# Making each head's softmax shift on GpSimd instead of VectorE, and turning and dividing its sums two units later

## The chip, the cores and the metric

One core of one Trainium2 chip. The metric is the device time of one launch in microseconds (us), the median of several runs. The profile is one execution of the program, taken by the hardware profiler. Engines: PE is TensorE (PEld its weight loads), DVE is VectorE, ACT is ScalarE, POOL is GpSimd, SP is SyncE, which issues DMAs here.

## The reference

A graph attention layer with a residual and a layer norm, then three relational graph convolutions with a residual and a layer norm, over 1250 nodes of 768 features and 40000 edges. The change lies in the attention alone:

```python
hh = h.reshape(n, 12, 64)
ft = jnp.einsum('nhd,ed->nhe', hh, W_fc)
a1 = jnp.einsum('nhd,hd->nh', ft, attn_l)
a2 = jnp.einsum('nhd,hd->nh', ft, attn_r)
e = jax.nn.leaky_relu(a1[src] + a2[dst], negative_slope=0.2)
m = jax.ops.segment_max(e, dst, num_segments=n)
ee = jnp.exp(e - m[dst])
denom = jax.ops.segment_sum(ee, dst, num_segments=n)
alpha = ee / denom[dst]
agg = jax.ops.segment_sum(alpha[:, :, None] * ft[src], dst, num_segments=n)
res = jnp.einsum('nhd,ed->nhe', hh, W_res)
return jax.nn.relu((res + agg).reshape(n, 12 * 64))
```

The maximum m only shifts the exponent: the kernel must take it from each node's incoming edges, and a node without edges must come out finite.

## The kernel before

A first stage counts the edges between each pair of nodes into dense matrices and projects the nodes; the last stage does the three convolutions as dense products. Neither is touched. Between them stands `attention`, which treats the graph as a dense matrix: for each of 12 heads (H) and each of 10 tiles (NT) of 125 source nodes (T) there is one **unit** u = head x 10 + tile, a matrix of 125 source nodes by 1250 destination nodes. The five engines run their own programs, written out by hand, and meet at semaphores. For unit u, in the order in which its data pass:

- `lift` (ACT, L644): y = relu(0.8 (a2 + a1)), 125x1250, into one of YS = 5 buffers. ACT lifts unit u + 4 behind the exponent of unit u, and waits until the pw of the buffer's last user is done.
- `bend` (POOL, L620), "the addition": y = y + lowb, where lowb is the shift of the head, spread over 125 partitions.
- `exponent` (ACT, L650): y = exp(y + a1_low).
- `weights` (DVE, L727), "pw": pw = min(y, 1) x edge counts, into one of 3 buffers.
- `gather` (PE, L791): six matmuls add x (64 features and a one) times pw into head_sums.

Once a head: `keep_sums` (ACT, L655) copies the sums out of PSUM behind exponent 1 of the next head, `turn_sums` (PE, L802) multiplies them by the projection, `divide` (DVE, L732 to L737) divides by the sum of weights into `share`, and `add` (POOL, L627), "the addition of a head", adds share to the result, behind the bend of unit 7.

The shift. `spread` (PE, L772) spreads a1 of a head over PSUM. `best` (DVE, L699), "the lookup", finds for one tile of destination nodes the largest a1 among their sources, one column of `tops` each; ten lookups give a head's maxima. DVE does the lookup of unit u + 20 beside the pw of unit u, two heads ahead; at tile 9 it stands before the pw, so that the lookups of tiles 8 and 9 follow each other. `lows` (DVE, L705 to L715) makes from the ten columns the shift 0.2 a2 - leaky(top + a2), with nodes without edges set to zero by a comparison with -GONE: four operations on 125x10 numbers, each behind a wait on the one before. `turn_low` (PE, L780) turns the 125x10 columns, `keep_low` (DVE, L721), "the row copy", copies them to SBUF, and SP writes them to memory and spreads them into `lowb` (L567, L571), two buffers. The order by hand puts lows(h + 2) behind the pw of tile 9 of head h, turn_low(h + 1) in front of the gather of tile 0, keep_low(h + 1) behind the pw of tile 0, turn_sums(h - 1) behind the gather of tile 0, divide(h - 1) behind the lookup of tile 3. Before unit 0, DVE does lows(0) behind ten lookups and lows(1) behind ten more; POOL waits only for the spread shift of head 0.

The tiles are named in the profile: y, pw, tops, bias_steps (the steps of the shift), low_cols (the shift), low_rows (turned), low_spread (lowb), head_sums, head_out, share, res. Buffer numbers are left out there (a2_col is a_col).

## Time and profile before

| | us |
|---|---|
| median of 3 runs (lowest, highest) | 2604.76 (2603.11, 2607.9) |
| the profiled execution's own time | 2603.86 |
| its span, first to last instruction | 2602.1 |
| PE busy | 2227.9 |
| DVE busy | 1376.9 |
| ACT busy | 785.4 |
| POOL busy | 540.9 |

The span is what the rows of the profile are placed in, from 0 us. A row of the timeline gives start and duration, engine, line and operation, output and inputs, and in brackets the idle time of the engine before it with the instruction that ended it. An engine that has taken up an instruction and waits for something inside the chip, not for a semaphore, counts as busy. Mean granted clock of PE over the span is 0.937 of full.

### The profile page before, as it was taken

The page shows a single profiled execution, that of the slowest core. Times are in us where ns is not written, and L with a number is a line of the kernel's source. Part 1 is how long each engine was busy: PE and PEld are TensorE (multiplying, and loading weights), DVE is VectorE, ACT ScalarE, POOL GpSimd, SP SyncE. Part 2 cuts the span into 40 slices and gives each one's busy share as a digit, 9 for nine tenths or more (in the row PEclk, how much of TensorE's full clock was granted, in tenths as well). Part 3 has the DMA queues.
Part 4 walks back from the last instruction along what each step waited for, and adds up shares of the span by engine and source line. Part 5 has one row for each costly group of instructions (what it writes and reads, how often), then busy time and mean ns, then how long its engine had stood idle before and what let it go on. Part 6 is the DMA issues. An engine that isn't in the chain of part 4 may idle for free.

```text
span 2602.1 us, 29664 instructions
## 1 busy us (share of the span) xinstructions
PE 2227.9 (86%) x10953; PEld 1849.4 (71%) x10954; DVE 1376.9 (53%) x1942; ACT 785.4 (30%) x1040; POOL 540.9 (21%) x224
## 2 busy tenths in 40 slices
PE   3997743777777745999999999999999989999997
PEld 1555531232323315999999989999999989999997
DVE  7886637999999956223333234232232242334335
ACT  0132222666666633112122133121121231212212
POOL 0000003989899930000000000000000000000000
PEclk9998875979889877999999999999999999999999
DMA  0133332211111043232343332333332342344332
GB/s 17 50 85 89 88 88 64 96 34 39 38 36 45 14 111 112 75 110 85 106 121 87 113 102 67 98 111 98 90 109 90 106 118 89 104 119 124 104 106 77
DMA packets 139392, 222.22 MB, mean 85 GB/s; under 512 B 86848, under 2 KB 87086, under 8 KB 139269
## 3 DMA queue, kind: packets, MB, share of 16 engines
q1 hardware_dynamic: 99935, 154.48, 20.9%
q0 software_dynamic: 39344, 66.16, 9.0%
q8 instruction: 80, 1.31, 0.2%
q14 instruction: 33, 0.27, 0.0%
HBM read 189.76 MB, written 30.56 MB: 85 GB/s over the span
## 4 chain that ended last, share of the span: by engine, by line
PE 55%; DMA 4%; DVE 2%; ACT 2%; issue 0%; SPq 0%; ACTq 0%; DVEq 0%
PE banks L1036 28%; PE banks L1008 26%; DMA w_raw<-in_L_gnn_w_root_dram 3%; DVE w_lo L1277 1%; ACT w_hi L1156 1%; DMA s_x<-x_tiles 1%; PE banks L1071 0%; DMA emb_raw<-in_L_gnn_w_rel_dram 0%; PE banks L1045 0%; PE banks L1058 0%; PE banks L1089 0%; DVE h_lo L1308 0%; DVE tail_stats L1327 0%; ACT accT L1184 0%; DVE back L1325 0%
## 5 line engine op out<-in xcount | busy, mean ns | idle before, releaser
L1008 PE MATMUL banks<-ct_in,h_hi 125*128 125x416 f32 (+1 forms) x1710 | 604.3, 353 | 0.6 <-ACT accT L1141 0.6
L1008 PE MATMUL banks<-ct_in,h_lo 125*128 125x416 f32 (+1 forms) x1710 | 603.1, 353 | 0.0
L1036 PE MATMUL banks<-g_hi,w_hi 128*128 128x416 f32 (+1 forms) x1440 | 515.9, 358 | 24.2 <-DVE g_lo L1299 24.2
L1036 PE MATMUL banks<-g_hi,w_lo 128*128 128x416 f32 (+1 forms) x1440 | 512.6, 356 | 0.0
L1036 PE MATMUL banks<-g_lo,w_hi 128*128 128x416 f32 (+1 forms) x1440 | 511.4, 355 | 0.0
L1277 DVE TENSOR_TENSOR w_lo<-w_raw,w_hi 128x768 fp32r<-128x768 f32 (+1 forms) x228 | 227.9, 1000 | 469.8 <-ACT w_hi L1156 469.8
L620 POOL TENSOR_TENSOR y<-y,low_spread 125x1250 f32<-125x1250 f32 x120 | 426.1, 3582 | 69.8 <-ACT y L644 38.0
L791 PE MATMUL head_sums<-pw,x 125*65 125x512 f32 x720 | 316.1, 587 | 101.9 <-DVE pw L727 100.7
L1156 ACT CAST w_hi<-w_raw 128x768 fp32r<-128x768 f32 (+1 forms) x228 | 197.9, 869 | 452.4 <-PE banks L1036 355.5
L1008 PEld LDWEIGHTS banks<-ct_in,h_lo 125*128 125x128 f32 x1710 | 323.7, 189 | 4.2
L1008 PEld LDWEIGHTS banks<-ct_in,h_hi 125*128 125x128 f32 x1710 | 322.4, 189 | 4.1 <-ACT accT L1141 0.8
L791 PEld LDWEIGHTS head_sums<-pw,x 125*65 125x65 f32 x720 | 102.2, 153 | 305.8 <-issue 170.7
L1287 DVE TENSOR_TENSOR gs<-banks,inv 128x416 f32<-128x416 f32 (+3 forms) x180 | 106.6, 592 | 392.4 <-PE banks L1008 392.3
L1172 ACT CAST g_hi<-gs 128x416 fp32r<-128x416 f32 (+3 forms) x180 | 97.5, 542 | 701.4 <-DVE gs L1287 701.4
L976 POOL DMA_DIRECT2D inv<-s_inv x27 | 15.4, 572 | 1386.6 <-DVE gs L1287 1372.9
L1036 PEld LDWEIGHTS banks<-g_hi,w_hi 128*128 128x128 f32 x1440 | 275.4, 191 | 33.2 <-DVE w_lo L1277 22.7
L727 DVE SCALAR_TENSOR_TENSOR pw<-y,csum 125x1250 f32<-125x1250 f32 x120 | 283.2, 2369 | 3.9 <-PE head_sums L791 2.8
L1036 PEld LDWEIGHTS banks<-g_lo,w_hi 128*128 128x128 f32 x1440 | 274.1, 190 | 4.7
L1036 PEld LDWEIGHTS banks<-g_hi,w_lo 128*128 128x128 f32 x1440 | 274.2, 190 | 3.3
L292 DVE TENSOR_SCALAR oh_key<-iota_key,edge_cols,minus_window 125x750 bf16<-125x750 uint16 x516 | 211.3, 474 | 80.4 <-PE win L417 55.3
L644 ACT ACTIVATE y<-a_spread,a_high 125x1250 f32<-125x1250 f32 x120 | 160.2, 1338 | 193.7 <-DVE pw L727 158.4
L417 PE MATMUL win<-oh_key,oh_rem 125*128 125x375 bf16 x1032 | 200.7, 340 | 11.1 <-issue 8.2
(175 smaller groups left out, 1592.9 us busy)
## 6 DMA issues: line engine op xcount, KB each, us to landing
w_raw<-in_L_gnn_w_rel_dram SPq DMA_DIRECT2D x117, 384.0 KB, 3.2
ct_in<-s_ct POOLq DMA_DIRECT2D x18, 2031.2 KB, 27.9
w_raw<-in_L_gnn_w_rel_dram SPq DMA_DIRECT2D x54, 448.0 KB, 4.2
ct_in<-s_ct POOLq DMA_DIRECT2D x9, 2041.0 KB, 28.9
s_ct<-ct_stage SPq DMA_DIRECT2D x30, 610.4 KB
w_raw<-in_L_gnn_w_root_dram SPq DMA_DIRECT2D x39, 384.0 KB, 3.3
w_raw<-in_L_gnn_w_root_dram SPq DMA_DIRECT2D x18, 448.0 KB, 5.8
a_spread<-s_a SPq DMA_DIRECT2D x12, 610.4 KB
```

The source lines that it names most:

```text
L292: nc.vector.tensor_scalar(oh_key[:, p, b], iota_key[:].rearrange("e s r d -> e (s r d)"), edge[:, 1, bass.ds(c, 1)], minus_w[:, bass.ds(w, ...
L417: ins = nc.tensor.matmul(win[:, p, m, 0:BANK * KEY], oh_rem[:, bass.ds(q, 1), :, b].rearrange("e q s -> e (q s)"), oh_key[:, p, b, m * BAN ...
L620: nc.gpsimd.tensor_tensor(y[:, u % YS], y[:, u % YS], lowb[:, h % 2], ALU.add).then_inc(bent, 1)
L644: nc.scalar.activation(y[:, u % YS], a2b[:, h % 2], ACT.Relu, scale=1.0 - SLOPE, bias=a1_high[:, s, h:h + 1]).then_inc(risen, 1)
L727: nc.vector.scalar_tensor_tensor(out=pw[:, u % 3], in0=y[:, u % YS], scalar=1.0, in1=csum[:, u % NT], op0=ALU.min, op1=ALU.mult).then_inc( ...
L791: ins = nc.tensor.matmul(po[:, o:o + w], x[:, s, h], pw[:, u % 3, o:o + w], start=s == 0, stop=s == NT - 1)
L1008: ins = nc.tensor.matmul(pb[0:rows, PA, 0:s.w], a, b, start=j == 0, stop=j == len(pairs) - 1)
L1036: ins = nc.tensor.matmul(pb[:, m, 0:s.w], a, b, start=s.first and j == 0, stop=s.last and j == len(parts) - 1)
L1156: nc.scalar.copy(w_hi[:, s.wi % WS, 0:s.mt * 128], w_raw[:, s.wi % 2, 0:s.mt * 128]).then_inc(w_hi_done, 1)
L1172: nc.scalar.copy(g_hi[0:rows, s.gi % 2, 0:s.w], gs[0:rows, 0:s.w]).then_inc(g_hi_done, 1)
L1277: nc.vector.tensor_tensor(w_lo[at], w_raw[:, s.wi % 2, 0:s.mt * 128], f32(w_hi[at]), ALU.subtract).then_inc(w_lo_done, 1)
L1287: nc.vector.tensor_tensor(gs[0:rows, 0:s.w], pb[0:rows, PA, 0:s.w], inv[0:rows, s.slab % 2, 0:s.w], ALU.mult).then_inc(gs_done, 1)
```

## The change

The shift is made by POOL. `lows` moves into POOL's program and is written there in operations on two tensors, or on one with constants: eight operations on 125x10 numbers in place of four, six steps buffers in place of three. The wait for the maxima stands in front of them. lows(0) and lows(1) stand before POOL's first bend; lows(h + 1) stands in front of the bend of tile 2 of head h, for h from 1 to 10. On PE, turn_low(h + 1) now stands behind the gather of tile 1, and turn_sums(h - 1) behind that of tile 2. On DVE, keep_low(h + 1) stands behind the pw of tile 2, and divide(h - 1) behind the lookup of tile 5. POOL's addition of a head stays behind bend 7.

```diff
--- before.py
+++ after.py
@@ -513,7 +513,7 @@
         wfc = sb("wfc", [HD, HD], F32)
         wfcT = sb("wfcT", [HD + 1, HD + 1], F32)
         tops = sb("tops", [T, NU], F32)
-        steps = sb("bias_steps", [T, 3, NT], F32)
+        steps = sb("bias_steps", [T, 6, NT], F32)
         low = sb("low_cols", [T, 2, NT], F32)
         row = sb("low_rows", [NT, T], F32)
         den = sb("den", [T, 2, NT // 2], F32)
@@ -626,8 +626,31 @@
                 at = res[:, :, h * HD:(h + 1) * HD]
                 nc.gpsimd.tensor_tensor(at, share[:].rearrange("p m t f -> p (m t) f"), at, ALU.add).then_inc(res_added, 1)
 
+            def lows(h):
+                a2, at, n = a2_col[:, :, h], [steps[:, j] for j in range(6)], h * 7
+                pool.wait_ge(maxed, (h + 1) * NT)
+                pool.wait_ge(low_ready, h)
+                nc.gpsimd.tensor_tensor(at[0], tops[:, h * NT:(h + 1) * NT], a2, ALU.add).then_inc(bias_step, 1)
+                nc.gpsimd.tensor_scalar(at[5], a2, SLOPE, None, ALU.mult).then_inc(bias_step, 1)
+                pool.wait_ge(bias_step, n + 1)
+                nc.gpsimd.tensor_scalar(at[1], at[0], 0.0, 1.0 - SLOPE, ALU.max, ALU.mult).then_inc(bias_step, 1)
+                nc.gpsimd.tensor_scalar(at[2], at[0], SLOPE, None, ALU.mult).then_inc(bias_step, 1)
+                pool.wait_ge(bias_step, n + 4)
+                nc.gpsimd.tensor_tensor(at[3], at[1], at[2], ALU.add).then_inc(bias_step, 1)
+                nc.gpsimd.tensor_scalar(at[4], at[0], -GONE, None, ALU.is_gt).then_inc(bias_step, 1)
+                pool.wait_ge(bias_step, n + 6)
+                nc.gpsimd.tensor_tensor(at[3], at[3], at[4], ALU.mult).then_inc(bias_step, 1)
+                pool.wait_ge(bias_step, n + 7)
+                if h >= 2:
+                    pool.wait_ge(low_turned, h - 1)
+                nc.gpsimd.tensor_tensor(low[:, h % 2], at[5], at[3], ALU.subtract).then_inc(low_ready, 1)
+
+            lows(0)
+            lows(1)
             for u in range(NU):
                 h, s = divmod(u, NT)
+                if s == 2 and 1 <= h and h + 1 < H:
+                    lows(h + 1)
                 bend(u)
                 if s == 7 and h:
                     add(h - 1)
@@ -699,22 +722,6 @@
                 nc.vector.tensor_tensor_reduce(junk[:, u % 2], a1[:, 0:N], nbr[:, t], 1.0, -NOEDGE / 10,
                                                ALU.subtract, ALU.max, tops[:, u:u + 1]).then_inc(maxed, 1)
 
-            def lows(h):
-                a2, at = a2_col[:, :, h], [steps[:, n] for n in range(3)]
-                dve.wait_ge(maxed, (h + 1) * NT)
-                nc.vector.tensor_tensor(at[0], tops[:, h * NT:(h + 1) * NT], a2, ALU.add).then_inc(bias_step, 1)
-                dve.wait_ge(bias_step, h * 3 + 1)
-                nc.vector.scalar_tensor_tensor(out=at[1], in0=at[0], scalar=SLOPE, in1=at[0],
-                                               op0=ALU.mult, op1=ALU.max).then_inc(bias_step, 1)
-                dve.wait_ge(bias_step, h * 3 + 2)
-                nc.vector.scalar_tensor_tensor(out=at[2], in0=at[1], scalar=-GONE, in1=at[1],
-                                               op0=ALU.is_gt, op1=ALU.mult).then_inc(bias_step, 1)
-                dve.wait_ge(bias_step, h * 3 + 3)
-                if h >= 2:
-                    dve.wait_ge(low_turned, h - 1)
-                nc.vector.scalar_tensor_tensor(out=low[:, h % 2], in0=a2, scalar=SLOPE, in1=at[2],
-                                               op0=ALU.mult, op1=ALU.subtract).then_inc(low_ready, 1)
-
             def keep_low(h):
                 dve.wait_ge(low_turned, h + 1)
                 dve.wait_ge(low_out, 16 * h)
@@ -739,28 +746,24 @@
 
             for t in range(NT):
                 best(t)
-            lows(0)
             best(NT)
             best(NT + 1)
             keep_low(0)
             node_tables()
             for t in range(2, NT):
                 best(NT + t)
-            lows(1)
             for u in range(NU):
                 h, s = divmod(u, NT)
                 more = h + 2 < H
                 if s == NT - 1 and more:
                     best(u + 2 * NT)
                 weights(u)
-                if s == 0 and h + 1 < H:
+                if s == 2 and h + 1 < H:
                     keep_low(h + 1)
                 if s < NT - 1 and more:
                     best(u + 2 * NT)
-                if s == 3 and h:
+                if s == 5 and h:
                     divide(h - 1)
-                if s == NT - 1 and more:
-                    lows(h + 2)
             divide(H - 1)
 
         @block.tensor
@@ -814,12 +817,12 @@
             spread(2)
             for u in range(NU):
                 h, s = divmod(u, NT)
-                if s == 0 and h + 1 < H:
-                    turn_low(h + 1)
                 if s == NT - 1 and h + 3 < H:
                     spread(h + 3)
                 gather(u)
-                if s == 0 and h:
+                if s == 1 and h + 1 < H:
+                    turn_low(h + 1)
+                if s == 2 and h:
                     turn_sums(h - 1)
             turn_sums(H - 1)
```

DVE at a boundary of heads: the pw of tile 9 (the second L699 in front of it is its lookup), then the next head. Before:

```order
L699 ISA junk,tops<-a_spread,nbr 125x1250 [waits maxed,a1_set]
L699 ISA tops 125x1
L727 SCALAR_TENSOR_TENSOR pw<-y,csum 125x1250 [waits summed_e,raised]
L705 TENSOR_TENSOR bias_steps<-tops,a_col 125x10 [waits maxed]
L707 SCALAR_TENSOR_TENSOR bias_steps<-bias_steps 125x10 [waits bias_step]
L710 SCALAR_TENSOR_TENSOR bias_steps<-bias_steps 125x10 [waits bias_step]
L715 SCALAR_TENSOR_TENSOR low_cols<-a_col,bias_steps 125x10 [waits low_turned,bias_step]
L727 SCALAR_TENSOR_TENSOR pw<-y,csum 125x1250 [waits summed_e,raised]
L721 COPY low_rows<-head_out 10x125 [waits low_out,low_turned]
L699 ISA junk,tops<-a_spread,nbr 125x1250 [waits maxed,a1_set]
L699 ISA tops 125x1
L727 SCALAR_TENSOR_TENSOR pw<-y,csum 125x1250 [waits summed_e,raised]
```

and with the change (pw is L734, the lookup L722, the row copy L728):

```order
L722 ISA junk,tops<-a_spread,nbr 125x1250 [waits maxed,a1_set]
L722 ISA tops 125x1
L734 SCALAR_TENSOR_TENSOR pw<-y,csum 125x1250 [waits summed_e,raised] x2
L722 ISA junk,tops<-a_spread,nbr 125x1250 [waits maxed,a1_set]
L722 ISA tops 125x1
L734 SCALAR_TENSOR_TENSOR pw<-y,csum 125x1250 [waits summed_e,raised]
L722 ISA junk,tops<-a_spread,nbr 125x1250 [waits maxed,a1_set]
L722 ISA tops 125x1
L734 SCALAR_TENSOR_TENSOR pw<-y,csum 125x1250 [waits summed_e,raised]
L728 COPY low_rows<-head_out 10x125 [waits low_out,low_turned]
L722 ISA junk,tops<-a_spread,nbr 125x1250 [waits maxed,a1_set]
```

The four operations between the two pw are gone, so these follow each other, and the row copy stands two pw further on.

POOL in heads 1 and 2, before (L620 is the bend, L627 the addition of a head; head 2 begins where low_in0 is waited for):

```order
L620 TENSOR_TENSOR y<-y,low_spread 125x1250 [waits low_in1,risen]
L620 TENSOR_TENSOR y<-y,low_spread 125x1250 [waits risen] x7
L627 TENSOR_TENSOR res<-share,res 125x10x64 [waits res_in,shared]
L620 TENSOR_TENSOR y<-y,low_spread 125x1250 [waits risen] x2
L620 TENSOR_TENSOR y<-y,low_spread 125x1250 [waits low_in0,risen]
L620 TENSOR_TENSOR y<-y,low_spread 125x1250 [waits risen] x7
```

and with the change, from the first bend of head 1:

```order
L620 TENSOR_TENSOR y<-y,low_spread 125x1250 [waits low_in1,risen]
L620 TENSOR_TENSOR y<-y,low_spread 125x1250 [waits risen]
L633 TENSOR_TENSOR bias_steps<-tops,a_col 125x10 [waits low_ready,maxed]
L634 TENSOR_SCALAR bias_steps<-a_col 125x10
L636 TENSOR_SCALAR bias_steps<-bias_steps 125x10 [waits bias_step]
L637 TENSOR_SCALAR bias_steps<-bias_steps 125x10
L639 TENSOR_TENSOR bias_steps<-bias_steps 125x10 [waits bias_step]
L640 TENSOR_SCALAR bias_steps<-bias_steps 125x10
L642 TENSOR_TENSOR bias_steps<-bias_steps 125x10 [waits bias_step]
L646 TENSOR_TENSOR low_cols<-bias_steps 125x10 [waits low_turned,bias_step]
L620 TENSOR_TENSOR y<-y,low_spread 125x1250 [waits risen] x6
L627 TENSOR_TENSOR res<-share,res 125x10x64 [waits res_in,shared]
```

Eight operations stand between the second and the third bend of the head, all others where they were.

PE at a boundary of heads, before: the gather of tile 9, the turned shift, the gather of tile 0, the turned sums:

```order
L791 MATMUL head_sums<-pw,x 65x512 [waits weighed]
L791 MATMUL head_sums<-pw,x 65x512
L791 MATMUL head_sums<-pw,x 65x226
L780 MATMUL head_out<-ident,low_cols 10x125 [waits shared,low_kept,low_ready]
L791 MATMUL head_sums<-pw,x 65x512 [waits o_kept,x_in1,weighed]
L791 MATMUL head_sums<-pw,x 65x512
L791 MATMUL head_sums<-pw,x 65x226
L802 MATMUL head_out<-wfcT,oT 125x65 [waits shared,low_kept,o_kept]
L802 MATMUL head_out<-wfcT,oT 125x65 x9
```

and with the change (the gather is L794, the turned shift L783, the turned sums L805), from the gather of tile 0:

```order
L794 MATMUL head_sums<-pw,x 65x512 [waits o_kept,x_in1,weighed]
L794 MATMUL head_sums<-pw,x 65x512
L794 MATMUL head_sums<-pw,x 65x226
L794 MATMUL head_sums<-pw,x 65x512 [waits weighed]
L794 MATMUL head_sums<-pw,x 65x512
L794 MATMUL head_sums<-pw,x 65x226
L783 MATMUL head_out<-ident,low_cols 10x125 [waits shared,low_kept,low_ready]
L794 MATMUL head_sums<-pw,x 65x512 [waits weighed]
L794 MATMUL head_sums<-pw,x 65x512
L794 MATMUL head_sums<-pw,x 65x226
L805 MATMUL head_out<-wfcT,oT 125x65 [waits shared,low_kept,o_kept]
L805 MATMUL head_out<-wfcT,oT 125x65 x9
```

The turned shift stands behind the gather of tile 1 and the turned sums behind that of tile 2.

## Rows read from the trace of the kernel before

**Rows 1.** The page: busy tenths in 40 slices of 65 us, DVE and POOL.
```profile
DVE  7886637999999956223333234232232242334335
...
POOL 0000003989899930000000000000000000000000
```

**Rows 2.** Busy time in a stretch: PE, PEld, DVE, ACT, POOL; clock, DMA, GB/s.
```profile
554.00:596.00 42.00, 35.55 (x88) 14.90 (x89) 41.83 (x39) 27.23 (x22) 38.36 (x12) 0.76 0.13 38
```

**Rows 3.** Timeline, DVE and POOL: start us, us, engine, line, operation, shapes.
```profile
620.99 2.27 DVE L727 SCALAR_TENSOR_TENSOR pw<-y,csum 125x1250 f32<-125x1250 f32 x1
623.18 1.45 DVE L699 CUSTOM_DVE_ANT_0 junk<-a_spread,nbr 125x1250 bf16<-125x1250 f32 x1
...
625.00 0.82 DVE L737 TENSOR_TENSOR share<-head_out,rden 125x640 f32<-125x640 f32 x1
...
647.51 2.81 DVE L705 TENSOR_TENSOR bias_steps<-tops,a_col 125x10 f32<-125x10 f32 x1
650.36 2.31 DVE L707 SCALAR_TENSOR_TENSOR bias_steps<-bias_steps 125x10 f32<-125x10 f32 x1
...
653.00 1.46 DVE L727 SCALAR_TENSOR_TENSOR pw<-y,csum 125x1250 f32<-125x1250 f32 x1
...
655.90 3.75 POOL L620 TENSOR_TENSOR y<-y,low_spread 125x1250 f32<-125x1250 f32 x1 [3.26 <-ACT y L644]
```

**Rows 4.** Timeline, POOL, additions of heads 4 and 5.
```profile
632.26 7.63 POOL L620 TENSOR_TENSOR y<-y,low_spread 125x1250 f32<-125x1250 f32 x2
...
639.85 12.80 POOL L620 TENSOR_TENSOR y<-y,low_spread 125x1250 f32<-125x1250 f32 x4
```

**Rows 5.** Timeline, DVE, the divisions of heads 10 and 11 and the end.
```profile
873.60 0.82 DVE L737 TENSOR_TENSOR share<-head_out,rden 125x640 f32<-125x640 f32 x1
...
913.09 0.82 DVE L737 TENSOR_TENSOR share<-head_out,rden 125x640 f32<-125x640 f32 x1
913.83 15.53 DVE L727 SCALAR_TENSOR_TENSOR pw<-y,csum 125x1250 f32<-125x1250 f32 x6
```

**Rows 6.** The row copy by source, 520 to 870 us: ns, first and last start.
```profile
L721 DVE COPY low_rows<-head_out x9: 270/270/271, 528.9 to 864.0; 10x125 f32<-10x125 f32 x9
```

**Rows 7.** Timeline, POOL: small operations, and an addition without pw.
```profile
5.64 0.12 POOL L198 MEMSET noedge_bias<- 125x1 f32 x1
5.68 0.22 POOL L199 MEMSET zero_a<- 125x128 bf16 x1
...
397.44 0.15 POOL L606 MEMSET emb_cols<- 128x67 f32 x1
397.65 1.13 POOL L608 MEMSET hot_rows<- 3x1250 f32 x1
...
433.86 2.40 POOL L620 TENSOR_TENSOR y<-y,low_spread 125x1250 f32<-125x1250 f32 x1
```

**Rows 8.** The head addition by source: ns min/median/max, first and last start.
```profile
L627 POOL TENSOR_TENSOR res<-share,res x12: 1531/2698/2768, 500.1 to 938.3; 125x640 f32<-125x640 f32 x12
```

**Rows 9.** Timeline, DVE and POOL, the start of head 0.
```profile
439.69 0.07 DVE L699 DVE_READ_ACCUMULATOR2_ANT tops<- 125x1 f32 x1
...
431.08 13.09 POOL L620 TENSOR_TENSOR y<-y,low_spread 125x1250 f32<-125x1250 f32 x5 [31.71 <-DMA low_spread<-s_low]
```

**Rows 10.** Timeline, DVE and POOL, head 0 to head 1.
```profile
482.69 1.45 DVE L727 SCALAR_TENSOR_TENSOR pw<-y,csum 125x1250 f32<-125x1250 f32 x1
486.81 0.28 DVE L721 COPY low_rows<-head_out 10x125 f32<-10x125 f32 x1 [2.66 <-PE head_out L780]
...
483.53 2.88 POOL L620 TENSOR_TENSOR y<-y,low_spread 125x1250 f32<-125x1250 f32 x1 [2.77 <-ACT y L644]
```

**Rows 11.** Timeline, PE: gathers of a unit, and the last ones.
```profile
637.69 2.31 PE L791 MATMUL head_sums<-pw,x 125*65 125x512 f32 x6 [1.70 <-DVE pw L727]
...
857.27 4.43 PE L791 MATMUL head_sums<-pw,x 125*65 125x512 f32 x6 [4.04 <-DVE pw L727]
...
926.67 6.51 PE L791 MATMUL head_sums<-pw,x 125*65 125x512 f32 x18 [1.26 <-DVE pw L727]
```

## The prediction

> **What bounds the kernel now.** The page comes first. In its 40 slices POOL is at 8 or 9 tenths in seven in a row, and DVE is at 9 there too [rows 1]: the attention stage, some 397 to 940 us, the only place the diff touches. Outside it nothing changes, so the sum is about this stage alone. There a stretch of 42 us, about a head, shows DVE busy for 41.83 and POOL for 38.36 us, PE for 35.55 and ACT for 27.23 [rows 2]. Two engines that are full side by side ask for the timeline. In it one weights operation (pw, L727) takes 1.46 us when POOL stands still and 2.27 us while POOL adds; the lookup for the maxima (L699) takes 1.45 us beside an addition [rows 3]. An addition of POOL (L620) takes 7.63 / 2 = 3.8 us where each meets a pw, and 12.80 / 4 = 3.2 us where only half of them do [rows 4]. So pw and the addition take turns at something they share, and nothing else does. I call it the port. The next look is the period: from 632.26 to 639.85 POOL starts two additions [rows 4], so a unit (one addition, one pw) costs 3.80 us of port. From the addition's end to pw's it is 1.3 us, which leaves 2.5 for POOL. That is the bound: not an engine but the turn-taking.
>
> How much of a head is port? In heads 10 and 11 there are neither lookups nor a new shift between the two divisions, and they are 913.09 - 873.60 = 39.49 us apart [rows 5]: ten units, and 1.49 for the addition of a head (L627, 1.4 us of port) and its hand-over. In the full heads the row copy L721 comes 9 times between 528.9 and 864.0 [rows 6]: 41.89 us a head. So 2.40 us a head are lost to the port. The boundary shows where: the first two shift operations stand in DVE for 2.81 and 2.31 us, waiting for a turn that they need for a moment, while POOL does two additions; then the y ring is empty, POOL waits 3.26 us for ACT's lift, which waits for pw [rows 3], and the port lies free for all of it but the 1.45 us of pw (L727 at 653.00), some 1.8 us, and for 0.35 us before that pw.
>
> **The change, part by part.** (1) Four DVE operations a head go (L705 to L715). They stand for 5.49 us in DVE (647.51 to 653.00) [rows 3], though only 2.15 us of that is port left idle later; the rest were turns in which POOL worked. Worth up to 2.40 us in each of the heads, all that is above 39.49.
>
> (2) Eight POOL operations a head come, of 125x10, each pair behind a wait on POOL's own result. Their port turns are short, but they run one behind another and the additions queue behind them. In that time DVE can use the port only if a pw is ready. Two are (the last of a head and the first of the next stand together in DVE's order now), and POOL waits for them, which is useful work. What is left, s, is port time lost. The trace has no such operation. From below: a memset and the next, which waits for it, start 0.21 us apart (L606, L608); without a wait they start 0.04 us apart (L198, L199) [rows 7]. Half of the eight wait. Four of each kind make 1.0 us; with only a memset's own 0.12 to 0.15 us for a waiting one it is 0.7. From above: the line through L627 alone (640 elements, 1.53 us [rows 8]) and the addition alone (1250, 2.40 us [rows 7]) leaves 0.62 us for an operation with no elements; eight make 5 us. With an addition of 2.88 us, one that starts after an idle [rows 10], it leaves 0.11 us, 0.9 us for eight. 
>
> (3) One more term comes with it: the addition behind the small ones starts after an idle (2.88, not 2.5 us [rows 10]): 0.35 us. A head then costs 39.49 + 1.3 + 0.35 = 41.14 us, 0.75 less than before.
>
> (4) The lead. POOL runs up to four additions ahead of DVE. Before, head 0 began its additions at 431.08, while DVE was still at the lookups of head 1; five were done at 444.17, just as the first pw became ready [rows 9]. Now the shift of head 1 stands in front of the first addition and needs the last of those lookups, which ends at 439.76 [rows 9]. POOL starts its additions at 439.76 + 1.3 = 441.1, has two done at 446.3, the first pw ends at 447.7, the ninth 8 x 3.80 later at 478.1. Two lookups in a row let POOL add twice (483.1), then come the pw of unit 9 (484.4), one small operation and that of head 1, unit 0: 486.0. Before, it ended at 482.69 + 1.45 = 484.14 [rows 10], and POOL was at its fifth addition of head 1 by then (the one at 483.53 that waits for the lift), three further on. Ten heads of 41.14 give 897.4 for the first pw of head 11. From there eight units and one more pw (31.8) and 1.5 for the addition of a head: 930.7. Before, the last pw ended at 929.36 [rows 5]. PE finished its backlog 3.8 us later (933.18) [rows 11]; now the last three pw come less bunched, 0.6 us back. The sum is **+0.7 us**: the gain of ten heads pays for the lead that is given up. Both ends are absolute times, so nothing is counted twice.
>
> (5) turn_low stands behind the gather of unit 1 now, keep_low behind the pw of unit 2. At 2.4 GHz a gather takes 2.31 us in a unit of 3.80 [rows 11], so unit 1's is over 1.5 us before pw 2 ends: free. At 1.2 GHz (the granted clock averages 0.76 of full in the stretch [rows 2]) a gather takes 4.43 us [rows 11] and DVE could wait some 2 us at keep_low, as it did once before, 2.66 us at 486.81 [rows 10]. I take nothing: the pause of 4.04 us in front of the last gather of a head, behind which the slow gather stands [rows 11], gets shorter.
>
> (6) turn_sums and divide go two units back, three units apart as before; POOL's head addition, still behind bend 7, now needs a division that comes after pw 5. While POOL is one addition ahead, bend 7 runs (2.2 to 2.7 us) beside lookup 5 and the division (2.57 us from pw's end to share's, 623.26 to 625.83 [rows 3]): no wait, as before. I take nothing, since the small operations of (2) bring the lead down to one in each head.
> (7) Loads, steps and semaphores: three more rows of 10 numbers in bias_steps; SP's order is unchanged, and from the row copy at unit 2 to the first use of the shift there are eight units less POOL's lead, over 20 us.
>
> The profiled execution took 2603.9 us around its span of 2602.1 and lies 0.9 us under the median of 2604.8. With +0.7 and a little for (5), I predict **2606 us**. About 0.2%, 5.2 us, is what a measurement of this kernel can tell from no change. The sum moves by 11 us for 1 us of s: it is slower than that from s = 1.7, faster below s = 0.75.
>
> **The rivals.** *Slower, POOL waits for the division.* If POOL comes to bend 7 two additions ahead, it has nothing to do until DVE is through lookup 5 and the division; the port is free for 2.57 us. For it: two lookups in a row at each boundary do give POOL a second addition, and the division was two units earlier before. Against: the eight operations take about one turn away again. It decides if POOL's lead at bend 7 is two or more. Price 2.6 us in ten heads: 2632 us. Chance 0.12.
> *Slower, the small operations are dear.* At 0.4 us each, between the two lines of (2), s = 3.2 and the time 2627 us. For it: the 1.53 us of L627 for half the elements of a 2.40 us addition [rows 7, 8]. Chance 0.13; the part of my own forecast with s just over 1.7 adds 0.02.
> *Faster, they hide or cost next to nothing.* If most of the eight slip through while pw 9 and pw 0 hold the port, s falls to 0.3 and the time to 2595 us. Against: L627 takes 1.53 us alone and 2.70 us in the median, so POOL operations that read do wait [rows 8]. Chance 0.08. Or they are cheap: if a waiting one takes no more than such a memset, s is the 0.7 us of (2) and the time 2599 us. For it: the 0.04 us between memsets [rows 7]; against: the 0.21 us with a wait. Chance 0.07.
> The section of the Trainium skill named in (2) leads to this last case.
> The change does what it says: the order shows the operations moved, so that is no rival of its own.
>
> **How the numbers follow.** Forecast 0.58 (within 5.2 us), faster 0.08 + 0.07 = 0.15, slower 0.12 + 0.13 + 0.02 = 0.27. The range leaves out the waiting division and the upper half of the dear operations at one end and half of the fast cases at the other: 2597 (s near 0.5) to 2619 (s near 2.4).
>
> **What would show it.** Right: the shift's operations on POOL in about 1.3 us plus waits of 1.4 us for pw; no 3.26 us idle of POOL at the boundary; L721 about 41.1 us apart; first addition at 441; DVE no longer at 41.8 of 42 but idle for short pieces, waiting for y; the last pw near 931. Wrong: an idle of 2 us and more in front of L627, waiting for share, a start-to-start time of the small operations far from 0.16 us, DVE waiting at the row copy for PE, or a lead that is won back.

## The result, and the profile after the change

| | before | after |
|---|---|---|
| time, median (us) | 2606.22 (2603.11 to 2607.90) | 2628.16 (2625.96 to 2631.24) |
| ratio after / before | | 1.0086 (95%: 1.0069 to 1.0104) |
| profiled execution: own time / span | 2603.9 / 2602.1 | 2627.3 / 2625.5 |
| first pw of head 0, of head 1, of head 11 ends | 445.97, 484.14, 901.55 | 447.77, 486.33, 915.11 |
| last pw ends | 929.36 | 948.06 |
| last addition of a head ends | 939.79 | 959.28 |

The kernel became 22 us slower. The forecast was 2606 with a range up to 2619: a miss, and not a close one. Of all the launches behind the numbers below, one of e1_add_late took 9581.64 us where its others took 2607.5 to 2611.5 us; it is left out of the interval, and why it was slow is not known. Here and below, "a head" is the time from the end of the pw of tile 0 to the end of the next one, read from the timelines. The busy tenths of the page after the change are the first place where it shows, beside [rows 1].

```profile
DVE  7886637988888846323233334232232342334335
...
POOL 0000003999999950000000000000000000000000
```

DVE has come down from 9 to 8 tenths in the attention stage and POOL has gone up to 9 in each slice: the work has moved as the diff says. Two stretches, a short head and a long one, say so in us. The columns are those of [rows 2].

```profile
554.00:596.00 42.00, 31.08 (x91) 11.93 (x89) 37.20 (x35) 27.45 (x21) 41.28 (x21) 0.92 0.14 40
596.00:640.00 44.00, 32.78 (x87) 12.41 (x86) 38.08 (x35) 26.64 (x21) 39.71 (x20) 0.84 0.11 34
```

POOL is now the engine with no room in the first (41.28 of 42), and has lost 4.3 us of 44 in the second. The row copy (by source; it answers to [rows 6]) gives the mean, and the head addition by source (it answers to [rows 8]) says what POOL lost:

```profile
L728 DVE COPY low_rows<-head_out x8: 270/270/277, 537.2 to 841.2; 10x125 f32<-10x125 f32 x8
```

```profile
L627 POOL TENSOR_TENSOR res<-share,res x12: 1530/2696/2775, 509.5 to 957.7; 125x640 f32<-125x640 f32 x12
its engine sat idle before it (us, times) until:
  DVE share L744: 33.1, 8
```

(841.2 - 537.2) / 7 = 43.43 us a head between these two copies, where 41.14 was forecast. POOL stands 33.1 us in front of the head addition, waiting for the division. The timelines break that up: five times 3.96 us, in heads 4, 5, 7, 8 and 9; twice 0.39 us, in heads 1 and 3; and the rest in front of the last one, where nothing queues behind. The ten heads from head 1 on last

41.30, 41.82, 41.30, **44.66, 43.79**, 41.83, **43.80, 44.66, 43.80**, 41.82 us.

So there are two kinds. The five short ones have a mean of 41.61, the five long ones (exactly those with the wait of 3.96 us) of 44.14. That is 2.53 us more, five times, 12.7 us. The small operations themselves are the other surprise. They stand in POOL's timeline at the start of head 0, where nothing disturbs them, with the addition behind them:

```profile
439.24 0.21 POOL L633 TENSOR_TENSOR bias_steps<-tops,a_col 125x10 f32<-125x10 f32 x1 [23.24 <-DVE tops L722]
439.42 0.26 POOL L634 TENSOR_SCALAR bias_steps<-a_col 125x10 f32<-125x10 f32 x1
439.64 0.28 POOL L636 TENSOR_SCALAR bias_steps<-bias_steps 125x10 f32<-125x10 f32 x1
...
440.21 0.20 POOL L639 TENSOR_TENSOR bias_steps<-bias_steps 125x10 f32<-125x10 f32 x1
...
441.11 0.21 POOL L646 TENSOR_TENSOR low_cols<-bias_steps 125x10 f32<-125x10 f32 x1
441.28 9.19 POOL L620 TENSOR_TENSOR y<-y,low_spread 125x1250 f32<-125x1250 f32 x3
```

The eight take s = 441.28 - 439.24 = 2.04 us, 0.26 us each, not the 1.3 us of term (2).

**How a long head comes about.** The timeline of head 4, whose boundary is at 602 to 616 us, PE first, then ACT, DVE and POOL:

```profile
603.05 4.43 PE L794 MATMUL head_sums<-pw,x 125*65 125x512 f32 x6 [4.04 <-DVE pw L734]
607.41 4.53 PE L775 MATMUL a_spread<-a_rows,ident 12*125 12x512 f32 x6
611.87 4.32 PE L794 MATMUL head_sums<-pw,x 125*65 125x512 f32 x6
...
616.23 1.20 ACT L678 COPY oT<-head_sums 65x1250 f32<-65x1250 f32 x1 [4.26 <-PE head_sums L794]
...
600.73 2.27 DVE L734 SCALAR_TENSOR_TENSOR pw<-y,csum 125x1250 f32<-125x1250 f32 x1 [2.71 <-ACT y L673]
...
611.98 1.46 DVE L722 CUSTOM_DVE_ANT_0 junk<-a_spread,nbr 125x1250 bf16<-125x1250 f32 x1 [1.22 <-PE a_spread L775]
...
619.92 3.08 DVE L734 SCALAR_TENSOR_TENSOR pw<-y,csum 125x1250 f32<-125x1250 f32 x1 [1.93 <-ACT y L673]
...
636.36 0.82 DVE L744 TENSOR_TENSOR share<-head_out,rden 125x640 f32<-125x640 f32 x1
637.10 1.45 DVE L734 SCALAR_TENSOR_TENSOR pw<-y,csum 125x1250 f32<-125x1250 f32 x1
...
612.48 20.82 POOL L620 TENSOR_TENSOR y<-y,low_spread 125x1250 f32<-125x1250 f32 x6
637.26 2.69 POOL L627 TENSOR_TENSOR res<-share,res 125x640 f32<-125x640 f32 x1 [3.96 <-DVE share L744]
```

Read it as a chain. (a) In front of the pw of tile 8 DVE waits 2.71 us for ACT's exponent: bend 8 stands behind the addition of a head, and DVE is through the units before it sooner than POOL. (b) So PE has nothing to gather for 4.04 us, in front of gather 8. From head 2 on this pause stands at every boundary, 4.04 to 4.05 us. The kernel before has no pause of that length in front of gather 8: with POOL four additions ahead, PE's pauses there were 1.3 to 1.7 us, those at the spread and at gather 9 0.4 and 1.2 us, and 4.04 us in front of gather 9 at one boundary alone, that of head 10, where no spread is left to be made [rows 11]. (c) From 602 on the granted clock is at half speed: gather 8, the spread for the lookups of a later head and gather 9 take 4.43, 4.53 and 4.32 us, and the three end 13.1 us after the pause (616.19), where DVE and ACT need them. (d) DVE's lookup waits 1.22 us for the spread; ACT's copy of the sums waits 4.26 us for gather 9, and the exponent of tile 2 stands behind that copy. (Before, that copy was done early: in heads 2 to 10 it started 2.3 to 3.5 us before the pw of tile 0 ended.) (e) The pw of tile 2 starts 9.16 us after that of tile 0 ended (610.76). (f) POOL goes on meanwhile, is done with bend 7 at 633.30, two additions ahead, and stands until the division, which now comes behind the pw of tile 5, has ended. From 634.61 to 637.10 nobody uses the port: 2.49 us, the length of the excess.

The short head before it, same views, 41.3 us earlier, has the same pause and another clock:

```profile
561.75 3.78 PE L794 MATMUL head_sums<-pw,x 125*65 125x512 f32 x6 [4.05 <-DVE pw L734]
565.47 2.36 PE L775 MATMUL a_spread<-a_rows,ident 12*125 12x512 f32 x6
568.13 4.01 PE L794 MATMUL head_sums<-pw,x 125*65 125x512 f32 x6 [0.30 <-DVE pw L734]
...
572.17 1.20 ACT L678 COPY oT<-head_sums 65x1250 f32<-65x1250 f32 x1 [1.50 <-PE head_sums L794]
...
576.08 2.72 DVE L734 SCALAR_TENSOR_TENSOR pw<-y,csum 125x1250 f32<-125x1250 f32 x1 [2.45 <-ACT y L673]
...
592.61 2.70 POOL L627 TENSOR_TENSOR res<-share,res 125x640 f32<-125x640 f32 x1 [0.39 <-DVE share L744]
```

Busy time of the two boundaries, with the columns of [rows 2]:

```profile
560.00:574.00 14.00, 10.56 (x20) 3.51 (x21) 13.63 (x12) 8.59 (x8) 13.67 (x12) 0.76 0.00 0
602.00:616.00 14.00, 12.95 (x18) 4.26 (x18) 12.78 (x10) 6.28 (x5) 13.67 (x12) 0.51 0.00 0
```

In the short one the clock came back for the spread (2.36 us), fell again for gather 9, and is 0.76 over the boundary, against 0.51, which is 1.2 GHz, all through the long one. ACT's copy starts 2.71 us after the pw of tile 0 ended (569.46), not 5.47 us, the pw of tile 2 starts 6.62 us after it, and POOL, whose bend 7 ends at the same distance in both (22.8 and 22.5 us), stands 0.39 us. Each of the five long heads follows a boundary with one piece of 13.7 us at the low level; each short one follows pieces of 3.4 or 6.8 us.

### The profile page after: what moved, and what is told of

Its sections match the earlier page's. It is cut to its first block, busy times and chain, and to the rows that moved or that the text cites. A ratio compares the mean times of both kernels' runs of the same rounds, so it can differ in the third digit from the quotient of the medians.

```text
span 2625.5 us, 29724 instructions
## 1 busy us (share of the span) xinstructions
PE 2230.7 (85%) x10953; PEld 1845.1 (70%) x10954; DVE 1331.2 (51%) x1894; ACT 788.0 (30%) x1040; POOL 570.2 (22%) x320
## 4 chain that ended last, share of the span: by engine, by line
PE 55%; DMA 4%; DVE 2%; ACT 1%; issue 0%; SPq 0%; ACTq 0%; DVEq 0%
PE banks L1039 28%; PE banks L1011 25%; DMA w_raw<-in_L_gnn_w_root_dram 3%; DVE w_lo L1280 1%; ACT w_hi L1159 1%; DMA s_x<-x_tiles 1%; PE banks L1074 0%; DMA emb_raw<-in_L_gnn_w_rel_dram 0%; PE banks L1048 0%; PE banks L1061 0%; PE banks L1092 0%; DVE h_lo L1311 0%; DVE tail_stats L1330 0%; ACT accT L1187 0%; DVE back L1328 0%
## 5 line engine op out<-in xcount | busy, mean ns | idle before, releaser
L1039 PE MATMUL banks<-g_hi,w_hi 128*128 128x416 f32 (+1 forms) x1440 | 516.8, 359 | 22.5 <-DVE g_lo L1302 22.5
L794 PE MATMUL head_sums<-pw,x 125*65 125x512 f32 x720 | 316.9, 585 | 137.8 <-DVE pw L734 122.1
L620 POOL TENSOR_TENSOR y<-y,low_spread 125x1250 f32<-125x1250 f32 x120 | 404.0, 3401 | 0.0
L794 PEld LDWEIGHTS head_sums<-pw,x 125*65 125x65 f32 x720 | 100.7, 153 | 348.5 <-issue 184.4
L734 DVE SCALAR_TENSOR_TENSOR pw<-y,csum 125x1250 f32<-125x1250 f32 x120 | 289.7, 2421 | 64.6 <-ACT y L673 63.6
L673 ACT ACTIVATE y<-y,a_low 125x1250 f32<-125x1250 f32 x120 | 159.8, 1331 | 137.7 <-POOL y L620 137.6
```

Source lines behind the costliest of these rows:

```text
L620: nc.gpsimd.tensor_tensor(y[:, u % YS], y[:, u % YS], lowb[:, h % 2], ALU.add).then_inc(bent, 1)
L673: nc.scalar.activation(y[:, u % YS], y[:, u % YS], ACT.Exp, bias=a1_low[:, s, h:h + 1]).then_inc(raised, 1)
L734: nc.vector.scalar_tensor_tensor(out=pw[:, u % 3], in0=y[:, u % YS], scalar=1.0, in1=csum[:, u % NT], op0=ALU.min, op1=ALU.mult).then_inc( ...
L794: ins = nc.tensor.matmul(po[:, o:o + w], x[:, s, h], pw[:, u % 3, o:o + w], start=s == 0, stop=s == NT - 1)
L1039: ins = nc.tensor.matmul(pb[:, m, 0:s.w], a, b, start=s.first and j == 0, stop=s.last and j == len(parts) - 1)
```

## The experiments

"After" is the changed kernel. Medians stand beside those of the kernel before on the same chip. Where the text compares two medians of different chips, the difference is good to some 2 us: counted from each chip's own kernel before, e1 is 17.5 us under after, not 19.3, e2 12.1, e5 4.6 and e6 17.2 us; e4 is 21.8 us above e1 and e7 7.1 us below it. The last two columns are of the profiled execution.

| run | us | before | ratio (95%) | heads 1 to 10, us | last pw |
|---|---|---|---|---|---|
| after | 2628.16 | 2606.22 | 1.0086 (1.0069, 1.0104) | 41.3 to 44.7 | 948.06 |
| e1_add_late | 2608.91 | 2604.50 | 1.0015 (1.0005, 1.0025) | 40.9 to 41.9 | 933.06 |
| e2_old_order | 2614.35 | 2604.50 | 1.0035 (1.0025, 1.0045) | 41.1 to 42.1 | 936.40 |
| e3_order_only | 2640.56 | 2604.50 | 1.0139 (1.0116, 1.0162) | 45.5, two of 49.4 and 47.0, 34.0 | 965.32 |
| e5_warm | 2621.85 | 2604.50 | 1.0059 (1.0042, 1.0076) | 41.8, six of 43.7 or 44.5 | 950.01 |
| e6_warm2 | 2610.65 | 2605.86 | 1.0015 (1.0006, 1.0025) | 41.3 and 41.8 | 934.77 |
| e4_double_small | 2632.11 | 2605.86 | 1.0084 (1.0067, 1.0101) | 42.8 to 43.7 | 953.91 |
| e7_lead | 2603.13 | 2605.86 | 0.9985 (0.9975, 0.9996) | 41.0 to 41.9 | 926.68 |
| e8_psum_steps | 2591.67 | 2605.86 | 0.9934 (0.9917, 0.9951) | 39.4 to 40.9, last 37.1 | 914.17 |
| e9_psum_two | 2588.62 | 2605.91 | 0.9930 (0.9915, 0.9944) | 39.4 to 40.9, last 37.1 | 911.12 |
| e10_sbuf_seven | 2611.46 | 2605.91 | 1.0026 (1.0016, 1.0035) | 42.4 and 42.7, first 44.8, last 34.7 | 937.53 |

**Is it the wait for the division?** Three runs: the addition of a head later, the old places with the new shift, and the new places with the old shift.

**e1_add_late**, against after:

```diff
                 bend(u)
-                if s == 7 and h:
+                if s == 9 and h:
                     add(h - 1)
```

> The changed kernel, with POOL's addition of a head behind bend 9 instead of bend 7. Chain theory (half of the heads are 2.5 us longer because POOL stands 3.96 us in front of this addition, two bends ahead of the division, and the late bend 8 leaves PE a pause of 4 us): the wait is gone in all heads, the pause in front of the gather of tile 8 too, the clock stays at 2.4 GHz for most of the boundary, every head takes 41.3 to 41.6 us, total about 2613 us. Price theory (the eight small operations, 2.04 us a head, and the lost lead explain all): 2628 us, heads as before, since the small operations are untouched.

Measured: 2608.91 us, 19 less than after. In heads 1 to 10 POOL never waits for share (among the waits between 480 and 945 us it is there once, 8.8 us, in front of the last addition), and the last pw ends 15.0 us earlier. The wait of rival 1 was there and it cost what the heads show.

**e2_old_order**, against after (on PE, DVE):

```diff
-                if s == 2 and h + 1 < H:
+                if s == 0 and h + 1 < H:
                     keep_low(h + 1)
...
-                if s == 5 and h:
+                if s == 3 and h:
                     divide(h - 1)
...
+                if s == 0 and h + 1 < H:
+                    turn_low(h + 1)
...
-                if s == 1 and h + 1 < H:
-                    turn_low(h + 1)
-                if s == 2 and h:
+                if s == 0 and h:
                     turn_sums(h - 1)
```

> The shift on POOL as in the change, but turned shift, row copy, turned sums and division where they were before the change (tiles 0, 0, 0 and 3). Chain theory: the division is long done when POOL comes to the addition of a head; no 3.96 us waits; the turned shift may hold PE for some us at tile 0, since POOL makes the shift only in front of bend 2. Heads of 41.5 to 42, total 2612 to 2617 us. Price theory: 2628 us.

Measured: 2614.35 us, 14 less than after; no wait for share over 0.39 us. Its boundaries tell something more. Twice its clock lies low for as long as in a long head, as in this stretch:

```profile
644.00:658.00 14.00, 13.05 (x19) 4.35 (x19) 8.64 (x7) 6.20 (x6) 13.67 (x12) 0.52 0.00 0
```

and the head behind it takes 42.00 us, with POOL even four additions ahead of DVE at tile 2. So the low clock costs nothing where the division comes early enough; the loss takes both. DVE waits at the row copy instead, 34.2 us in ten times, while POOL adds: the ten heads have a mean of 41.69 us, e1's 41.41.

**e3_order_only**, against before:

```diff
-                if s == 0 and h + 1 < H:
+                if s == 2 and h + 1 < H:
                     keep_low(h + 1)
...
-                if s == 3 and h:
+                if s == 5 and h:
                     divide(h - 1)
...
-                if s == 0 and h + 1 < H:
-                    turn_low(h + 1)
...
-                if s == 0 and h:
+                if s == 1 and h + 1 < H:
+                    turn_low(h + 1)
+                if s == 2 and h:
                     turn_sums(h - 1)
```

> The kernel before, with only the new places of turned shift, row copy, turned sums and division; the shift stays on DVE. Chain theory: POOL is four bends ahead here, so it waits for the division in every head, some 6 us, in which two pw use the port: 2.5 to 3.5 us lost a head, 44.5 to 45.5 us a head, total 2630 to 2640 us. Price theory: the order is harmless without the small operations, 2606 us.

Measured: 2640.56 us, 36 more than before. The head addition by source, and a line of POOL's timeline:

```profile
its engine sat idle before it (us, times) until:
  DVE share L737: 82.5, 11
```

```profile
643.49 2.69 POOL L627 TENSOR_TENSOR res<-share,res 125x640 f32<-125x640 f32 x1 [6.72 <-DVE share L737]
```

With the shift on DVE, POOL is four additions ahead at tile 2 of heads 1 to 10 and stands 6.7 us in most. The new places are bad by themselves; in after the small operations keep POOL to two or three ahead, which spares it part of that.

**Is it the clock?** e5 and e6 give PE something to multiply while it has nothing to gather: small products into unused columns of PSUM, read by nobody.

**e5_warm**, against after, in front of `gather(u)`:

```diff
+                if s == 8:
+                    for _ in range(10):
+                        nc.tensor.matmul(pf[0:T, 0, 384:384 + T], ident[0:T, 0:T], ident[0:T, 0:T], start=True, stop=True)
```

> The changed kernel with ten matmuls of 125x125 into unused PSUM columns in front of the gather of tile 8 of each head, where PE pauses 4 us; their results are not used. Chain theory: the clock no longer falls to 1.2 GHz for 13.7 us at every second boundary, ACT's copy of the sums is never late, POOL does not get its third bend ahead of pw 2, the 3.96 us waits vanish, heads 41.3 to 41.8 us, total about 2615 us. Rival, that the lead grows whatever the clock does: 2628 us, heads of 44 us with the clock at full.

Measured: 2621.85 us, 6 less than after in the median; but its last pw ends at 950.01, 1.9 us later than after's, so no gain in the attention stage is shown. Filling one pause is not enough. PE's timeline at a boundary (L824 is the filling):

```profile
563.12 2.34 PE L824 MATMUL head_out<-ident 125*125 125x125 f32 x20
567.34 2.32 PE L794 MATMUL head_sums<-pw,x 125*65 125x512 f32 x6 [1.88 <-DVE pw L734]
570.10 2.36 PE L775 MATMUL a_spread<-a_rows,ident 12*125 12x512 f32 x6 [0.44 <-DVE tops L722]
573.71 4.43 PE L794 MATMUL head_sums<-pw,x 125*65 125x512 f32 x6 [1.25 <-DVE pw L734]
```

Gather 8 and the spread are fast again, 2.3 us, but three shorter pauses remain, and the clock falls at gather 9 instead, for 10.2 us. Six heads are long, and again exactly those in which POOL waits 3.96 us; each has such a piece of 10.2 us at the low level in front. (A seventh piece stands in front of head 10, which has no lookups left and is short.) But the way from the clock to the wait is another one than in after. ACT's copy is 0.6 to 0.7 us late (3.13 us behind the end of the pw of tile 0, where the short heads 4, 6 and 8 have 2.4 to 2.6), and the pw of tile 2 starts 6.8 to 7.1 us behind it in long and short heads alike. It is DVE's row copy that waits, for the turned shift, which stands on PE behind the gathers 9, 0 and 1, the first of them slow (4.43 us above):

```profile
585.76 0.28 DVE L728 COPY low_rows<-head_out 10x125 f32<-10x125 f32 x1 [1.39 <-PE head_out L783]
```

1.1 to 1.5 us in each of the six long heads and in head 10, nothing in the three short ones between them. The low clock makes DVE late by one wait or by another; in both runs the loss comes when POOL then stands for the division.

**e6_warm2**, against after, in the same place:

```diff
+                for _ in range({8: 12, 9: 5, 0: 5}.get(s, 0)):
+                    nc.tensor.matmul(pf[0:T, 0, 384:384 + T], ident[0:T, 0:T], ident[0:T, 0:T], start=True, stop=True)
```

> The changed kernel with filling matmuls (results not used) in all three pauses of PE at a boundary: 12 in front of the gather of tile 8, 5 in front of those of tiles 9 and 0. In the run with one filled pause the clock still fell for 10 us at six boundaries, and those heads were the long ones. Clock theory: with the clock at 2.4 GHz at all boundaries no head waits 3.96 us for the division, heads 41.3 to 41.8, total 2613 to 2616 us. Rival: the clock and the long heads only go together by chance; long heads stay, 2622 to 2628 us.

Measured: 2610.65 us, 17.5 less than after, by work that computes nothing; 13.3 us of it are in the attention stage (the last pw). Busy time of the stage, PE, PEld, DVE, ACT, POOL and granted clock, in e6:

```profile
480.00:945.00 465.00, 374.02 (x1469) 187.25 (x1467) 392.64 (x339) 295.56 (x228) 447.82 (x202) 0.95 0.13 38
```

and in after:

```profile
480.00:945.00 465.00, 342.74 (x942) 130.30 (x940) 399.33 (x335) 290.64 (x226) 441.12 (x201) 0.88 0.12 38
```

The ten heads are 41.31 and 41.85 in turn, no wait for share in them is over 0.39 us, and no low piece at a boundary is longer than 6.8 us. The division stands where it stood in after. The row copy waits once, 0.7 us. So the clock is the second condition, shown from its side. That the mean clock decides nothing is shown by the kernel before, which has 0.86 in the same stretch and no long head but the first.

**What do the small operations cost?** **e4_double_small**, against e1: seven of the eight operations once more, into the same buffers.

```diff
+                nc.gpsimd.tensor_tensor(at[0], tops[:, h * NT:(h + 1) * NT], a2, ALU.add).then_inc(bias_step, 1)
+                nc.gpsimd.tensor_scalar(at[5], a2, SLOPE, None, ALU.mult).then_inc(bias_step, 1)
+                pool.wait_ge(bias_step, n + 8)
...
```

> The kernel with POOL's addition behind bend 9 (e1, 2608.9 us), in which seven of the eight small operations of each shift are done twice, with the same values; 15 operations in place of eight. If the serial time of the small operations is lost port time (2.04 us for eight), each head gets 1.8 us longer, and the start too: 20 us more, 2629 us. Rival, that they are mostly hidden beside pw: up to 3 us more, 2612 us.

Measured: 2632.11 us, 23 more than e1. Its heads have a mean of 43.25, e1's 41.41: 1.84 us a head for seven operations, 0.26 each, as in the eight of after at the start. Seven more behind the first seven lengthen the head one for one. Whether a part of the first eight hides beside the pw of tiles 9 and 0, the case of the third rival, this run does not separate; if it does, it is little, since a short head of after is 0.3 us under its sum (below).

**What is the lead worth?** **e7_lead**, against e1: the shift of head 1 inside head 0.

```diff
-            lows(1)
...
-                if s == 2 and 1 <= h and h + 1 < H:
+                if s == (4 if h == 0 else 2) and h + 1 < H:
                     lows(h + 1)
```

> The kernel with POOL's addition behind bend 9 (e1), with the shift of head 1 made behind bend 3 of head 0 instead of in front of bend 0, so that POOL adds from 431 us on. If the lead given up at the start is worth its port time (three bends of 2.5 us), 7 us less than e1, 2602 us, and the first pw starts at 444.5 or earlier. Rival, the lead is lost again at the first boundaries because the y ring empties or the division is waited for: 2607 to 2609 us.

Measured: 2603.13 us. POOL starts its additions at 429.94, the first pw ends at 441.57, the other heads are as in e1, and the last pw ends 6.4 us earlier. It is the first version of the change that is not slower than before.

**Is the port what DVE's four operations waited for?** If it is, they need not leave DVE: it is enough that none has both inputs in SBUF. **e8_psum_steps**, against before, keeps the shift on DVE and puts its steps into unused columns of the PSUM tile of a1:

```diff
-                a2, at = a2_col[:, :, h], [steps[:, n] for n in range(3)]
+                a2, at, n = a2_col[:, :, h], [a1[:, 1280 + 16 * j:1280 + 16 * j + NT] for j in range(4)], h * 6
...
-                nc.vector.tensor_tensor(at[0], tops[:, h * NT:(h + 1) * NT], a2, ALU.add).then_inc(bias_step, 1)
...
+                dve.wait_ge(a1_set, min(h + 2, H))
+                nc.vector.tensor_copy(at[0], tops[:, h * NT:(h + 1) * NT]).then_inc(bias_step, 1)
+                dve.wait_ge(bias_step, n + 1)
+                nc.vector.tensor_tensor(at[1], at[0], a2, ALU.add).then_inc(bias_step, 1)
+                dve.wait_ge(bias_step, n + 2)
+                nc.vector.tensor_scalar(steps[:, 0], at[1], 0.0, 1.0 - SLOPE, ALU.max, ALU.mult).then_inc(bias_step, 1)
...
```

> The kernel before, with the shift still on DVE but in seven operations of which none reads two tensors from SBUF (one input lies in unused PSUM columns each time). Port theory: these never wait for POOL's additions, 1.5 us a head in DVE in place of 5.5; the y ring doesn't empty; heads 40.0 to 40.8 us in place of 41.9, total 2588 to 2596 us. Rival, DVE itself is the bound and what counts is its number of operations: 2604 us or more.

Measured: 2591.67 us, 14 less than before. DVE's timeline at a boundary:

```profile
644.00 0.16 DVE L706 COPY a_spread<-tops 125x10 f32<-125x10 f32 x1
644.20 0.18 DVE L708 TENSOR_TENSOR a_spread<-a_spread,a_col 125x10 f32<-125x10 f32 x1
644.40 0.17 DVE L710 TENSOR_SCALAR bias_steps<-a_spread 125x10 f32<-125x10 f32 x1
...
645.23 0.17 DVE L721 SCALAR_TENSOR_TENSOR low_cols<-a_col,a_spread 125x10 f32<-125x10 f32 x1
```

and POOL's:

```profile
650.69 10.85 POOL L620 TENSOR_TENSOR y<-y,low_spread 125x1250 f32<-125x1250 f32 x3 [0.33 <-ACT y L644]
```

Seven operations in 1.4 us, none waiting for POOL; and POOL's idle of 3.26 us at the boundary [rows 3] is 0.33. Heads 2 to 9 take (846.45 - 528.59) / 8 = 39.73 us, where the prediction read 39.49 us as a head's port work [rows 5]: of the 2.40 us lost, 0.24 are left.

**e10_sbuf_seven** is the control: the same seven operations and waits, with all steps in SBUF.

```diff
-                a2, at, n = a2_col[:, :, h], [a1[:, 1280 + 16 * j:1280 + 16 * j + NT] for j in range(4)], h * 6
+                a2, at, n = a2_col[:, :, h], [steps[:, 2 + j] for j in range(4)], h * 6
```

> Control for e8: the same seven operations on DVE in the same places and with the same waits, but all steps in SBUF, so that three of them read two tensors from SBUF. Port theory: these three, and perhaps those that copy from SBUF to SBUF, wait for a bend each; POOL runs out of lifted units as in the kernel before or earlier; heads 42 to 45 us, total 2605 to 2635 us. Rival, that e8 gained by something else (another rounding of the order, the wait for the spread): 2592 us.

Measured: 2611.46 us, 5.6 more than before and 20 more than e8. DVE's timeline:

```profile
609.64 2.36 DVE L706 COPY bias_steps<-tops 125x10 f32<-125x10 f32 x1
612.04 2.75 DVE L708 TENSOR_TENSOR bias_steps<-bias_steps,a_col 125x10 f32<-125x10 f32 x1
614.83 0.17 DVE L710 TENSOR_SCALAR bias_steps<-bias_steps 125x10 f32<-125x10 f32 x1
```

The same copy takes 2.36 us instead of 0.16, the same sum 2.75 instead of 0.18. (The five operations behind them take 0.17 us each, also those with two inputs in SBUF: POOL has run out of lifted units at 614.76 and stands until 618.64, so there is nothing to wait for.) Where the operands lie is all that differs between the two runs, so it is the port. The Trainium skill (SBUF — State Buffer, section "SBUF: two separate sides") describes such a port: DVE and GpSimd hold a shared pair exclusively, for a whole instruction, and DVE asks for it with two SBUF inputs or in a 2-port mode. The sums agree (2.75 and 0.18 us); the copy has one input and waits too, 2.36 us, as the page has it for fp32 copies inside SBUF.

**e9_psum_two** is e8 with the shifts of heads 0 and 1 made as before, since e8's first pw ended 2.9 us late (448.87 against 445.97): at 446.09 its DVE has waited 4.69 us for the next spread, which the new copy needs.

```diff
+            def lows(h):
+                return lows_sbuf(h) if h < 2 else lows_psum(h)
```

> The run with the steps in PSUM (e8, 2591.7 us), but the shifts of heads 0 and 1 made as in the kernel before, since in e8 the first one waits for the spread of the next head (the first pw ended at 448.9 us in place of 446.0). Port theory: first pw end back at 446.0, heads as in e8, 2 to 3 us less, 2589 us. Rival: the start does not reach the end because the lead absorbs it, 2591 to 2592 us.

Measured: 2588.62 us (2582.09 to 2592.06), the last pw 3.1 us earlier than e8's; the two medians are 3.1 us apart as well, though the runs of the two overlap. It has the lowest median here, 17 us under before and 40 under after.

## Why the prediction was wrong

**Right.** The bound was read rightly: a turn-taking port, 39.49 us of it a head, 2.40 us lost (e8: 39.73; e10: the loss is back). The start of (4) came out: the first pw at 447.77 for 447.7, that of head 1 at 486.33 for 486.0. The tenth is luck: the small operations took 0.7 us more than assumed, and the last lookup ended at 439.16, 0.6 us sooner than the 439.76 carried over from before. Giving the early start up costs 6.4 us at the last pw (e7 against e1; 7 us had been expected there). POOL's 3.26 us idle at the boundary are gone. The tail behind head 11 was 32.95 us for 33.3.

**Wrong, step (6), the larger part: 12.7 us.** It said that the division two units later costs nothing, "since the small operations of (2) bring the lead down to one in each head". Nothing in the trace of before stood behind that sentence. The lead is what remains of a race that ACT and PE can interrupt on DVE's side. In five heads they did, POOL came to bend 7 two additions ahead, and rival 1 took place at the condition named for it ("two or more") and its price (2.6 us forecast, 2.53 measured), in five heads and not in ten. It had been given a chance of 0.12. e1, e2 and e3 show that wait; in e3, the order alone, the time grew by 36 us with it.

**Wrong, step (5).** "I take nothing: the pause of 4.04 us in front of the last gather of a head, behind which the slow gather stands [rows 11], gets shorter." The row was read as one of every head, and it is one of a single boundary, that of head 10; at the others no pause of PE from gather 8 to gather 0 was over 2.2 us. With the change there is a pause of 4.04 us at each boundary from head 2 on, in front of gather 8. Behind it stand three groups of PE's work before ACT's copy, and all three can be slow. The step looked for the slow gather at the row copy. There DVE waited 0.4 us in all in after (twice); the exponent of tile 2 hangs on ACT's copy of the sums, and that was late. In e5 it is the row copy that waits, 1.1 to 1.5 us in the long heads: the place was rightly named, and taken at nothing. e6 shows the clock as the cause by filling the pauses.

**Wrong, term (2): a size.** s is 2.04 us, not 1.3: 0.26 us an operation instead of 0.16. Over the ten heads that is 0.74 x 10 = 7.4 us; it was the second rival's direction, at two fifths of its size (0.10 us more an operation, not 0.24).
**A slip without weight.** Part (1) counts 2.15 us of port left idle at a boundary before. The 0.35 us in front of the pw lie inside POOL's idle time of 3.26 us and are counted twice; it is 1.8 us. Nothing in the sum uses the figure.

**The account.** Last pw: 930.7 forecast, 948.06 measured, 17.4 us later: 12.7 + 4.7, and a start and an end that cancel (+0.3, -0.35). From there to the end of the last addition 11.22 us instead of 10.43, +0.8. From there to the end of the span 1666.2 us instead of 1662.3, +3.9. Together 22.1 of the 22.2 us between the forecast (2605.1 in terms of the profiled execution) and its 2627.3.

**What stays open.** The 3.9 us behind the attention stage: from the last pw to the end of the span the profiled executions of before and of the ten experiments have between 1670.6 and 1678.2 us, in no order that their edits suggest, and after has 1677.4; it may differ from run to run, which was not tested. Why the medians of e1, e5 and e6 are further from after's than their last pw is open with it. Why e2 is 5.4 us above e1 in the median when its last pw is 3.3 us later is open too. So is why the low clock lasts 13.7 us at some boundaries and comes in pieces at others, with the same pause in front, 4.04 to 4.05 us: the runs show what follows from each, not what chooses.

## What to carry to other kernels

Where two engines take turns at a port, first ask whether the small operation between the large ones can be had without the port (one input in PSUM: -14 us here) before moving it to the other engine, which trades its wait for serial time on the bound (0.26 us an operation, eight of them a head). A step that is moved later on one engine has to be held against the fixed order of the engine that waits for its result, with that engine's lead taken at its largest, not its usual value: doing the same addition two bends later (e1) was free, and its last pw came 15.0 us sooner. And an engine that is idle for a quarter of the stage can still set the pace: list what stands behind its longest pause, at the low clock, up to each instruction that another engine needs (here ACT's copy in after, the row copy in e5). A row that is to stand for every head has to be looked up at more than one.

## What the runs showed of the hardware

- A POOL operation on 125x10 fp32 numbers takes 0.20 to 0.21 us with two tensor inputs and 0.24 to 0.28 us with one and constants, so the form with one input is the dearer. From start to start they are 0.17 to 0.34 us apart.
- A copy of 125x10 fp32 numbers on DVE waits for POOL when it goes from SBUF to SBUF (2.36 us) and does not when it goes to PSUM (0.16 us).
- PE is busy for 343 of 465 us of the stage, so it is not the engine that is full, and its low clock still costs there: with 22 filling matmuls a head the last pw ends 13.3 us sooner (e6 against after).
